# One selective scan in a fused layer: from 16 state rows over channels to tiles of 8 channels x 16 states, fed from DRAM and multiplied on GpSimd

## The chip, the cores and the metric

The kernel runs on one core of a Trainium2 chip. The metric is the time of one execution on the device, in microseconds (us): the median of three runs. Beside it there is one profiled execution, whose trace is what the rows below are read from. Engines are called PE (TensorE), DVE (VectorE), ACT (ScalarE), POOL (GpSimd) and SP (the queue that issues the transfers).

## The reference, cut to what matters

A layer of three parts runs over 16 sequences of 256 tokens with 128 channels: an attention with features instead of a softmax, a selective scan ("mixer") with a gated linear unit, and after each of them a feed-forward part with weights and activations rounded to FP4. The change is in the scan, and in one clip of the attention's features.

```python
exp_arg = jnp.clip(proj * sqrt_2s - s, -20.0, 20.0)      # attention: the clip
prf = jnp.exp(exp_arg) * inv_sqrt_m
...
def _selective_scan(u, dt, A, Bm, Cm, D):                # u, dt: [b, l, 256]; A: [256, 16]
    dA = jnp.exp(dt[..., None] * A)                      # decay
    dBu = (dt * u)[..., None] * Bm[:, :, None, :]        # drive; Bm, Cm: [b, l, 16]
    def step(h, inp):
        dA_t, dBu_t = inp
        h = dA_t * h + dBu_t
        return (h, h)
    ...
    y = jnp.einsum('lbdn,bln->bld', hs, Cm)              # read-out, summed over the 16 states
    return y + u * D
```

For each sequence that is 256 channels x 16 states = 4096 recurrences over 256 tokens.

## The kernel before, in words

A group is two sequences (512 tokens, `TOK`); there are 8 groups. The program is written out as ten turns of a software pipeline. A turn works on three groups at once: `new` (its attention), `mid` (attention's end, feed-forward A, mixer up to dt), `old` (the scan, mixer's end, feed-forward B). Each turn has two halves of 16 slots. In the first half DVE scans the old group while the feed-forward A of the middle group runs; in the second half the features, scores and context of the new group run, with the mixer of the middle group and feed-forward B of the old one. The order on every engine is the order of the code; engines meet at semaphores alone.

A sum over groups therefore has eight scan stretches: six in turns 2 to 7, which repeat with one period, one in turn 8 (no new group) and one in turn 9 (the last group alone, with some feed-forward work of the group before it).

The scan before lays 128 channels on the partitions and takes one state after the other. For each state `s`:

- `decay_in` (ACT, L705): exp(dt * -A) for both halves of the channels, from `dt` in SBUF into `decay`.
- `drive_by_token` (ACT, L717): dt*u, turned to tokens on partitions, times the B of that state.
- `drive` (PE, L1464): eight transposes bring it back into PSUM, banks 4 and 5.
- `scan` (DVE, L1147): two scans of 512 columns. Its first input `decay` is in SBUF, its second, the drive, is in PSUM; it writes `state` in SBUF.
- `read_out` (POOL, L623): `state` times the C of that state (`c_row`, loaded from DRAM to all partitions) into `read`, one multiply of 1024 columns. Before each of them `vector_rest` makes POOL wait until certain DVE instructions are done.
- `sum_states` (PE, L1480): the identity times `read`, summed over the states in banks 6 and 7.

Of the rest the text names: `features` (DVE), which clips `expf` (L1130) and multiplies it by `sqf` into `feat` (L1136); `hidden_*` and `ffn_input_*` (DVE), the rounding steps L1035, L1040, L1045, L1063 and L1116; `deviation` (POOL), which makes a normalisation's factors with a power (L559); the scaling of `qk` (DVE, L1219); the bias added to `xab` (POOL, L640) and the Newton step for `rnorm` (POOL, L648 to L657); `scale_hidden` (POOL, L576 to L585), which stands in the last turn only.

## Time and profile before

| | |
|---|---|
| median of 3 runs | 1380.71 us (1379.58 to 1384.39) |
| the profiled execution's own time | 1384.66 us |
| its span | 1382.6 us |
| busy share PE, DVE, ACT, POOL | 81%, 74%, 68%, 31% |
| instructions PE, DVE, ACT, POOL | 5421, 1576, 1829, 353 |
| moved by DMA | 41.11 MB, mean 30 GB/s |
| POOL's multiply by C (L623) | 128 times, 2359 ns each |
| DVE's scan (L1147) | 256 times, 1203 ns each |

The span runs from the first to the last instruction of the program; the profiled execution's own time is a little longer. Busy shares are means over the whole span, and the two halves of a turn differ: what limits one does not limit the other. An engine's idle time counts only where something later waits for it.

### The profile page before, as it was taken

Reading aid. Unit: us, or ns where it says so; the run is one execution under the profiler, and the core shown is the slowest. Engines: PE = TensorE matmul, PEld = TensorE weight load, DVE = VectorE, ACT = ScalarE, POOL = GpSimd, SP = SyncE. Lnnn points to the kernel's source line nnn. Section 1 sums busy time; section 2 is a strip of 40 time slices with the busy share of each in tenths; the row PEclk is TensorE's granted clock in tenths of the full one; section 3 lists DMA queues with packets and bytes.
Section 4 is the critical chain, followed back from the end, with each engine's and each line's share of the span. In section 5 each row is a group of like instructions: output and inputs, shape, how many; then the busy total and the mean of one; then the engine's idle time right before and its main releaser. Section 6 shows DMA issues by size and latency. Waiting matters only on the chain. (4 is left out here: it accounts for less than half of the span.)

```text
span 1382.6 us, 17127 instructions
## 1 busy us (share of the span) xinstructions
PE 1117.1 (81%) x5421; PEld 620.8 (45%) x5421; DVE 1018.5 (74%) x1576; ACT 937.3 (68%) x1829; POOL 422.6 (31%) x353
## 2 busy tenths in 40 slices
PE   3975788798888988898889888899779887856854
PEld 1343444444544455544544454544545454424423
DVE  1655658877897789887887789887887788646643
ACT  3443579767795769667886769577886768457721
POOL 3010106520354006520354006510443015404623
PEclk8786899999999999999999999999999999967885
DMA  2000012100110102101120002000110101000200
GB/s 73 1 3 6 1 32 61 40 1 32 32 62 15 32 1 69 39 1 32 33 67 8 32 1 77 31 1 32 39 54 9 32 15 62 23 32 28 60 12 8
DMA packets 31401, 41.11 MB, mean 30 GB/s; under 512 B 4617, under 2 KB 14674, under 8 KB 31314
## 3 DMA queue, kind: packets, MB, share of 16 engines
q1 hardware_dynamic: 31314, 40.02, 9.7%
q8 instruction: 46, 0.75, 0.2%
q14 instruction: 41, 0.34, 0.1%
HBM read 37.65 MB, written 2.36 MB: 29 GB/s over the span
## 5 line engine op out<-in xcount | busy, mean ns | idle before, releaser
L623 POOL TENSOR_TENSOR read<-state,c_row 128x1024 f32<-128x1024 f32 x128 | 300.4, 2359 | 280.0 <-DVE state L1147 107.8
L1147 DVE TENSOR_TENSOR_SCAN state<-decay,bank 128x512 f32<-128x512 f32 x256 | 296.2, 1203 | 56.5 <-PE bank L1464 47.5
L1480 PE MATMUL bank<-read,ident 128*128 128x512 f32 x512 | 258.8, 634 | 1.1 <-POOL read L623 1.1
L1464 PE MATMUL bank<-ident,drive_by_token 128*128 128x128 f32 x1024 | 167.7, 302 | 99.2 <-DVE state L1147 90.6
L717 ACT ACTIVATE drive_by_token<-dtu_t,b_t 128x256 f32<-128x256 f32 x512 | 217.3, 500 | 1.0 <-PE bank L1464 0.9
L1464 PEld LDWEIGHTS bank<-ident,drive_by_token 128*128 128x128 f32 x1024 | 124.2, 152 | 165.4 <-issue 108.6
L705 ACT ACTIVATE decay<-dt,neg_a 128x510 f32<-128x510 f32 x256 | 169.6, 713 | 12.5 <-DVE state L1147 12.5
L1405 PE MATMUL bank<-znt,omega 128*128 128x512 f32 x256 | 141.0, 633 | 22.1 <-ACT sqf L696 22.0
L1157 DVE TENSOR_TENSOR s_sb<-bank,causal 128x512 f32<-128x512 f32 x128 | 88.0, 688 | 78.0 <-PE bank L1418 77.8
L693 ACT ACTIVATE expf<-bank,minus_s,root2s 128x512 f32<-128x512 f32 x128 | 99.6, 778 | 65.7 <-PE bank L1405 64.7
L1480 PEld LDWEIGHTS bank<-read,ident 128*128 128x128 f32 x512 | 98.0, 208 | 86.3 <-issue 80.3
L1442 PE MATMUL bank<-s_sb,vext 128*32 128x256 f32 (+1 forms) x1024 | 128.8, 342 | 0.9 <-ACT s_sb L726 0.5
L551 POOL TENSOR_SCALAR a_ln_rstd<-a_ln_mv 128x4 f32<-128x4 f32 x8 | 1.6, 194 | 405.4 <-DVE a_ln_mv L1017 405.4
L1416 PE MATMUL bank<-feat 64*128 64x256 f32 x512 | 94.1, 430 | 16.1 <-ACT s_sb L726 16.1
L726 ACT ACTIVATE s_sb<-bank 128x256 f32<-128x256 f32 x128 | 49.3, 385 | 78.1 <-DVE s_sb L1157 78.1
L1136 DVE SCALAR_TENSOR_TENSOR feat<-expf,scale_f,sqf 128x512 f32<-128x512 f32 x128 | 96.2, 752 | 6.4 <-ACT sqf L696 0.5
L1442 PEld LDWEIGHTS bank<-s_sb,vext 128*32 128x32 f32 x1024 | 39.8, 110 | 92.6 <-issue 59.8
L1416 PEld LDWEIGHTS bank<-feat 64*128 64x128 f32 x512 | 42.5, 186 | 76.8 <-issue 61.2
L696 ACT ACTIVATE sqf<-bank 128x512 f32<-128x512 f32 x128 | 75.9, 593 | 0.0
L1130 DVE TENSOR_SCALAR expf<-expf 128x512 f32<-128x512 f32 x128 | 57.9, 452 | 18.1 <-ACT expf L693 17.6
L1405 PEld LDWEIGHTS bank<-znt,omega 128*128 128x128 f32 x256 | 43.6, 196 | 59.4 <-issue 54.3
L1418 PEld LDWEIGHTS bank<-feat 64*128 64x128 f32 x512 | 55.6, 191 | 3.6
(235 smaller groups left out, 1721.8 us busy)
## 6 DMA issues: line engine op xcount, KB each, us to landing
c_row<-c_rows SPq DMA_DIRECT2D x128, 256.0 KB, 3.2
xa<-x_dram SPq DMA_DIRECT2D x8, 256.0 KB, 3.8
out_dram<-x SPq DMA_DIRECT2D x8, 256.0 KB, 2.4
omega<-omega_t_dram SPq DMA_DIRECT2D x1, 512.0 KB
c_rows<-xdbl SPq DMA_DIRECT2D x8, 32.0 KB, 1.6
wqkv<-w_qkv_t_dram SPq DMA_DIRECT2D x1, 192.0 KB
state<-w_down_dram SPq DMA_DIRECT2D x1, 176.0 KB, 2.7
state<-w_gate_dram SPq DMA_DIRECT2D x1, 128.0 KB, 2.0
```

The costliest lines, as they stand in the source:

```text
L623: pool.tensor_tensor(read[:, s % STATE_BUFFERS], state[:, s % STATE_BUFFERS], c_row[:, s % C_BUFFERS].unsqueeze(1).broadcast_to([P, DT, TO ...
L693: act.activation(expf[:, s % 2], bank[:, 0], ACT.Exp, bias=minus_s[:], scale=root2s[:]).then_inc(exp_done.sem, 1)
L705: last = act.activation(decay[:, s % 2, k, :, 1:], dt[:, k].rearrange("p (b t) -> p b t", b=SEQS)[:, :, 1:], ACT.Exp, scale=neg_a[:, k, s: ...
L717: last = act.activation(by_token[:, s % DRIVES, t], dtu_t[:, t], ACT.Identity, scale=b_t[:, t, s:s + 1])
L1136: dve.scalar_tensor_tensor(feat[:, s % 2], expf[:, s % 2], scale_f[:], sqf[:, s % 2], ALU.mult, ALU.mult).then_inc(feat_done.sem, 1)
L1147: dve.tensor_tensor_scan(state[:, s % STATE_BUFFERS, c], decay[:, s % 2, c].rearrange("p b t -> p (b t)"), bank[:, DRIVE_BANK + c], 0.0, A ...
L1157: dve.tensor_tensor(s_sb[:, s % S_BUFFERS].rearrange("p h (k t) -> p h k t", t=P)[:, :, 0:3:2], bank[:, 1:3, 0:SEQ + P].rearrange("p h (k ...
L1405: pe.matmul(bank[:, 0], omega[:, j], znt[:, b], start=True, stop=True).then_inc(proj_ps.sem, 1)
L1416: pe.matmul(bank[:, 1 + h, 0:SEQ], f[:, SEQ:SEQ + P], f[:, 0:SEQ], start=True, stop=True)
L1442: last = pe.matmul(o, columns, scored, start=(k == 0 and below == 0), stop=(k == 1 and below == 1))
L1464: last = pe.transpose(bank[:, DRIVE_BANK + c, t * P:(t + 1) * P], by_token[:, s % DRIVES, t, c * P:(c + 1) * P], ident[:])
L1480: last = pe.matmul(bank[:, 6 + k], ident[:], read[:, s % STATE_BUFFERS, k], start=(s == 0), stop=(s == STATES - 1))
```

## The change

Eight channels x 16 states lie on the 128 partitions now, so one scan of 512 columns advances 8 channels with all their states. 32 such tiles cover the 256 channels; two of them make a span, and there are 16 spans for a group, one to a slot as the states were. The scans are as many as before and of the same length, but both their inputs lie in SBUF.

- `dt` and `dt*u` are stored to DRAM (`store_dt`), and each span loads its rows from there, each row to 16 partitions: `load_dt` into `decay`, `load_dtu` into `state`, 128 x 1024 each. B and C come from DRAM once for a group (`load_bc`).
- POOL multiplies a span by B in place (`drive`) and, after the scan, by C in place (`read_out`). The drives run `LEAD` = 5 spans ahead. `vector_rest` is gone.
- ACT makes the decay in place, and zeroes two columns first. Its multiply by B and PE's transposes of the drive are gone.
- PE sums the states with 0/1 tiles (`pick`) of 32 columns instead of the identity.
- The clip of `expf` stays on DVE for the first three slots (`CLIPS`) and is done on POOL in the other 13.
- dt is made on DVE in slot 10 instead of 12. Three small DVE instructions change their form (from one tensor input and two numbers to two tensor inputs).

```diff
@@ scan()
                 dve.wait_ge(decay_done.sem, decay_done.at(gb, s + 1))
-
-                dve.wait_ge(read_done.sem, read_done.at(gb, max(s + 1 - STATE_BUFFERS, 0)))
-                for c in range(DT):
-                    dve.wait_ge(drive_ps.sem, drive_ps.at(gb, DT * s + c + 1))
-                    dve.tensor_tensor_scan(
-                        state[:, s % STATE_BUFFERS, c],
-                        decay[:, s % 2, c].rearrange("p b t -> p (b t)"),
-                        bank[:, DRIVE_BANK + c], 0.0, ALU.mult, ALU.add).then_inc(
-                            (half_done if c == 0 else state_done).sem, 1)
+                dve.wait_ge(drive_done.sem, drive_done.at(gb, s + 1))
+                for e in range(2):
+                    span = state[:, s % STATE_BUFFERS, e]
+                    last = dve.tensor_tensor_scan(
+                        span, decay[:, s % DECAY_BUFFERS, e].rearrange("p b t -> p (b t)"), span,
+                        0.0, ALU.mult, ALU.add)
+                last.then_inc(state_done.sem, 1)
...
@@ GpSimd: drive, read_out, clip
+            def in_place(span, rows):
+
+                return pool.tensor_tensor(span, span, rows[:].unsqueeze(1).broadcast_to(
+                    [P, 2, TOK]), ALU.mult)
+
+            def drive(group, s):
+
+                landed = state_loaded[s % STATE_BUFFERS]
+                pool.wait_ge(bc_loaded.sem, bc_loaded.at(group, 2))
+                pool.wait_ge(landed.sem, landed.at(group, s // STATE_BUFFERS + 1))
+                in_place(state[:, s % STATE_BUFFERS], b_rows).then_inc(drive_done.sem, 1)
+
+            def read_out(group, s):
+
                 pool.wait_ge(state_done.sem, state_done.at(group, s + 1))
...
-                vector_rest(turn, s)
...
+                in_place(state[:, s % STATE_BUFFERS], c_rows).then_inc(read_done.sem, 1)
...
+            def clip(ga, s):
+
+                pool.wait_ge(exp_done.sem, exp_done.at(ga, s + 1))
+                pool.wait_ge(clipped.sem, clipped.at(ga, s))
+                pool.tensor_scalar(expf[:, s % 2], expf[:, s % 2], EXP_HIGH, EXP_LOW,
+                                   ALU.min, ALU.max).then_inc(clipped.sem, 1)
...
@@ SP: the loads of a span
+            def load_dt(group, s):
+
+                sp.wait_ge(dt_stored.sem, dt_stored.at(group, DT))
+                sp.wait_ge(state_done.sem, state_done.at(group, s + 1 - DECAY_BUFFERS))
+                slot = s % DECAY_BUFFERS
+                sp.dma_start(decay[:, slot].rearrange("p e b t -> p (e b t)"),
+                             span_rows(dt_dram, s)).then_inc(decay_loaded[slot].sem, 16)
...
@@ ACT: decay_in
+                act.activation(rows[:, :, 1, 0], rows[:, :, 1, 0], ACT.Copy, scale=0.0)
+                for e in range(2):
+                    last = act.activation(rows[:, e, :, 1:], rows[:, e, :, 1:], ACT.Exp,
+                                          scale=neg_a[:, tile_of(s, e):tile_of(s, e) + 1])
...
@@ PE: sum_states (and drive() is gone)
-                for k in range(DT):
-                    last = pe.matmul(bank[:, 6 + k], ident[:], read[:, s % STATE_BUFFERS, k],
-                                     start=(s == 0), stop=(s == STATES - 1))
+                k, q = divmod(s // 2, WIDE // CHANNELS)
+                for e in range(2):
+                    g = 2 * (s % 2) + e
+                    last = pe.matmul(bank[WIDE * g:WIDE * (g + 1), 6 + k], pick[:, q],
+                                     state[:, s % STATE_BUFFERS, e], start=(q == 0),
+                                     stop=(q == WIDE // CHANNELS - 1))
```

**The order on POOL.** These are POOL's instructions from the end of a second half into the next first half, in the kernel before: the factors of feed-forward B's and of the attention's normalisation, then the multiplies by C.

```order
156 L551 TENSOR_SCALAR b_ffn_ln_rstd<-b_ffn_ln_mv 128x4
157 L555 TENSOR_SCALAR b_ffn_ln_shift<-b_ffn_ln_mv 128x4
158 L559 TENSOR_TENSOR b_ffn_ln_rstd<-b_ffn_ln_rstd,minus_half 128x4
159 L566 TENSOR_TENSOR b_ffn_ln_shift<-b_ffn_ln_shift,b_ffn_ln_rstd 128x4
160 L551 TENSOR_SCALAR a_ln_rstd<-a_ln_mv 128x4
161 L555 TENSOR_SCALAR a_ln_shift<-a_ln_mv 128x4
162 L559 TENSOR_TENSOR a_ln_rstd<-a_ln_rstd,minus_half 128x4
163 L566 TENSOR_TENSOR a_ln_shift<-a_ln_shift,a_ln_rstd 128x4
164 L623 TENSOR_TENSOR read<-state,c_row 128x1024 x2
```

And the same place now:

```order
277 L700 TENSOR_SCALAR expf<-expf 128x512 x7
278 L649 TENSOR_TENSOR state<-state,b_rows 128x1024
279 L700 TENSOR_SCALAR expf<-expf 128x512
280 L649 TENSOR_TENSOR state<-state,b_rows 128x1024
281 L700 TENSOR_SCALAR expf<-expf 128x512
282 L649 TENSOR_TENSOR state<-state,b_rows 128x1024
283 L700 TENSOR_SCALAR expf<-expf 128x512
284 L649 TENSOR_TENSOR state<-state,b_rows 128x1024 x2
285 L649 TENSOR_TENSOR state<-state,c_rows 128x1024
286 L608 TENSOR_SCALAR a_ln_rstd<-a_ln_mv 128x4
```

The clips of slots 13, 14 and 15 stand behind the first three multiplies by B, and the attention's normalisation of the next group stands behind two more of them and one multiply by C.

**The order on DVE.** This is DVE at the end of the second half and the start of the first, in the kernel before; then now.

```order
616 L1040 SCALAR_TENSOR_TENSOR b_ffn_rounded<-b_ffn_magic,b_ffn_h 128x704
617 L1045 SCALAR_TENSOR_TENSOR b_ffn_rounded<-b_ffn_magic,b_ffn_rounded 128x704
618 L1116 TENSOR_TENSOR b_ffn_h<-b_ffn_rounded,b_ffn_qh_scale 128x704
619 L1147 SCALAR_TENSOR_TENSOR state<-decay,bank 128x512 x2
620 L1167 TENSOR_SCALAR rden<-bank 128x32
```

```order
551 L1074 SCALAR_TENSOR_TENSOR b_ffn_rounded<-b_ffn_magic,b_ffn_h 128x704
552 L1079 SCALAR_TENSOR_TENSOR b_ffn_rounded<-b_ffn_magic,b_ffn_rounded 128x704
553 L1150 TENSOR_TENSOR b_ffn_h<-b_ffn_rounded,b_ffn_qh_scale 128x704
554 L1181 SCALAR_TENSOR_TENSOR state<-decay,state 128x512 x4
555 L1200 TENSOR_SCALAR rden<-bank 128x32
```

Four scans stand there now instead of two (the scan is printed under its instruction's kind), and the second input of each is `state` instead of `bank`.

## Rows read from the trace of the kernel before

**Rows 1.** Busy time by half: a second half of a turn, then the next first half

```profile
core 0: us, PE busy (x) PEld busy (x) DVE busy (x) ACT busy (x) POOL busy (x), PEclk, DMA share, GB/s
591.00:669.70 78.70, 71.21 (x390) 35.97 (x388) 61.60 (x107) 57.88 (x106) 6.83 (x12) 0.98 0.05 15
669.70:744.60 74.90, 62.18 (x287) 38.71 (x288) 65.77 (x93) 58.37 (x123) 42.52 (x29) 0.95 0.18 50
...
1200.00:1280.00 80.00, 52.00 (x175) 28.20 (x174) 41.59 (x64) 48.99 (x92) 24.86 (x21) 0.72 0.09 27
```

**Rows 2.** DVE instructions with two SBUF inputs beside POOL: timeline, one turn

```profile
561.69 3.25 DVE L1219 TENSOR_TENSOR qk<-qk,rnorm 128x512 f32<-128x512 f32 x2
...
561.43 2.35 POOL L623 TENSOR_TENSOR read<-state,c_row 128x1024 f32<-128x1024 f32 x1
```

**Rows 3.** The same by line: duration ns min/median/max over the span

```profile
L1219 DVE TENSOR_TENSOR qk<-qk,rnorm x16: 678/686/2681, 29.8 to 1025.2; 128x512 f32<-128x512 f32 x16
...
L559 POOL TENSOR_TENSOR b_ffn_ln_rstd<-b_ffn_ln_rstd,minus_half x8: 1007/1523/1525, 309.8 to 1338.4; 128x4 f32<-128x4 f32 x8
...
L1147 DVE TENSOR_TENSOR_SCAN state<-decay,bank x256: 1186/1196/1222, 207.3 to 1320.6; 128x512 f32<-128x512 f32 x128
...
L623 POOL TENSOR_TENSOR read<-state,c_row x128: 2340/2358/2379, 214.9 to 1321.9; 128x1024 f32<-128x1024 f32 x128
```

**Rows 4.** POOL's and DVE's groups in one first half (busy us, mean ns)

```profile
L623 POOL TENSOR_TENSOR read<-state,c_row 128x1024 f32<-128x1024 f32 x16 | 37.5, 2357 | 26.9 <-DVE x L1124 6.5 <-DVE a_ffn_h L1116 6.2 <-DVE a_ffn_h L1035 4.6
L640 POOL TENSOR_TENSOR xab<-xa,bout 128x512 f32<-128x512 f32 x1 | 1.3, 1276 | 0.0
...
L1147 DVE TENSOR_TENSOR_SCAN state<-decay,bank 128x512 f32<-128x512 f32 x32 | 37.0, 1203 | 4.6 <-PE bank L1464 4.6
```

**Rows 5.** Busy time of tile newton_t, of tile a_ffn_rounded on DVE, of line L1035

```profile
669.70:744.60 74.90, 1.61 (x4) 0.95 0.18 50
...
669.70:744.60 74.90, 7.99 (x9) 0.95 0.18 50
...
669.70:744.60 74.90, 2.48 (x3) 0.95 0.18 50
```

**Rows 6.** The end of a second half: tile b_ffn_rounded, then a group of DVE

```profile
656.00:669.80 13.80, 2.68 (x3) 0.00 (x0) 0.88 0.00 0
...
L1136 DVE SCALAR_TENSOR_TENSOR feat<-expf,scale_f,sqf 128x512 f32<-128x512 f32 x2 | 1.5, 751 | 0.1
```

**Rows 7.** Timeline: DVE near the end of the second half; POOL's last multiply, two turns

```profile
645.89 0.68 DVE L1157 TENSOR_TENSOR s_sb<-bank,causal 128x512 f32<-128x512 f32 x1
...
589.51 2.35 POOL L623 TENSOR_TENSOR read<-state,c_row 128x1024 f32<-128x1024 f32 x1 [3.26 <-DVE state L1147]
...
743.14 2.35 POOL L623 TENSOR_TENSOR read<-state,c_row 128x1024 f32<-128x1024 f32 x1 [3.27 <-DVE state L1147]
```

**Rows 8.** Timeline of the last two turns: POOL, and DVE's dt*u

```profile
1202.53 2.34 POOL L623 TENSOR_TENSOR read<-state,c_row 128x1024 f32<-128x1024 f32 x1 [2.82 <-DVE state L1147]
...
1245.68 1.23 DVE L1338 TENSOR_TENSOR dtu<-dt,u 128x1024 f32<-128x1024 f32 x1
...
1266.72 2.60 POOL L576 TENSOR_SCALAR b_ffn_magic<-b_ffn_magic 128x704 bf16<-128x704 bf16 x1 [6.46 <-DVE b_ffn_rounded L1040]
...
1271.03 1.39 POOL L585 TENSOR_TENSOR b_ffn_h<-b_ffn_rounded,b_ffn_qh_scale 128x704 f32<-128x704 f32 x1
...
1321.86 2.34 POOL L623 TENSOR_TENSOR read<-state,c_row 128x1024 f32<-128x1024 f32 x1 [2.10 <-DVE state L1147]
```

**Rows 9.** Transfers: issues (KB each, us to landing), and the queue (packets, MB, share)

```profile
c_row<-c_rows SPq DMA_DIRECT2D x128, 256.0 KB, 3.2
...
out_dram<-x SPq DMA_DIRECT2D x8, 256.0 KB, 2.4
...
q1 hardware_dynamic: 31314, 40.02, 9.7%
```

**Rows 10.** POOL's one-input instruction of the Newton step, 128x128

```profile
L654 POOL TENSOR_SCALAR newton_t<-newton_t x8: 305/305/972, 28.9 to 1021.5; 128x128 f32<-128x128 f32 x8
```

More of the change, by code:

```diff
@@ new lines, in store_dt, with span_rows @@
+            def store_dt(group, values, dram, done, stored_in):
+                sp.wait_ge(done.sem, done.at(group, 1))
+                sp.wait_ge(state_done.sem, state_done.at(group, 0))
+                per = WIDE // CHANNELS
+                for k in range(DT):
+                    sp.dma_start(dram[per * k:per * (k + 1)].rearrange("q d g t -> g (q d) t"),
+                                 values[:, k]).then_inc(stored_in.sem, 16)
+            def span_rows(dram, s):
+                row = P // WIDE * TOK
+                return bass.AP(dram.tensor, s // 2 * CHANNELS * row + s % 2 * 2 * TOK,
+                               [[row, CHANNELS], [0, STATES], [1, 2 * TOK]])
@@ L492, in _ @@
                 if turn.has_old:
-                    for s in range(C_BUFFERS, 2 * C_BUFFERS):
-                        load_c(turn.old, s)
+                    for s in range(DECAY_BUFFERS, STATE_BUFFERS):
+                        load_dt(turn.old, s)
                 if i + 1 < GROUPS:
@@ L497, in _ @@
                 if turn.has_old:
-                    for s in range(2 * C_BUFFERS, STATES):
-                        load_c(turn.old, s)
+                    for s in range(STATE_BUFFERS, SPANS):
+                        load_dtu(turn.old, s)
+                        load_dt(turn.old, s)
                 if turn.is_last:
@@ L662, in body @@
                     attention_rest(turn, k)
-                    if turn.has_old:
-                        read_out(turn, k)
+                    if turn.has_old and k + LEAD < SPANS:
+                        drive(turn.old, k + LEAD)
+                    if turn.has_old and k + 1 < SPANS:
+                        read_out(turn.old, k + 1)
                 if turn.has_mid:
                     deviation(norm_b, turn.mid)
-                if turn.has_old:
-                    deviation(ffn_b.norm, turn.old)
+                for k in range(SLOTS):
+                    if turn.has_new and k >= CLIPS:
+                        clip(turn.new, k)
+                    if turn.has_old and k == 5:
+                        deviation(ffn_b.norm, turn.old)
+                    if turn.has_mid and k >= SLOTS - LEAD + 1:
+                        drive(turn.mid, k - (SLOTS - LEAD + 1))
+                if turn.has_mid:
+                    drive(turn.mid, LEAD - 1)
+                    read_out(turn.mid, 0)
                 if turn.is_last:
@@ L854, in mixer_early @@
                     ffn_ht(ffn_b, old, 0)
-                if turn.has_mid and k == 14:
-                    for h in range(DT):
-                        act.wait_ge(dtu_t_ps.sem, dtu_t_ps.at(mid, h + 1))
-                        act.activation(
-                            dtu_t[:, 2 * h:2 * h + 2].rearrange("p t c -> p (t c)"),
-                            bank[:, 4 + h], ACT.Copy).then_inc(dtu_t_done.sem, 1)
             def mixer_rest(turn, k):
@@ L1352, in body @@
                 for k in range(SLOTS):
-                    if turn.has_old and k > 0:
-                        scan(turn.old, k)
+                    if turn.has_old and 1 < k + 1 < SPANS:
+                        scan(turn.old, k + 1)
                     if turn.has_mid and k == 0:
@@ L1369, in body @@
                     mixer_rest(turn, k)
+                    if turn.has_mid and k == SLOTS - 1:
+                        scan(turn.mid, 0)
                 if turn.has_mid:
-                    scan(turn.mid, 0)
+                    scan(turn.mid, 1)
                 if turn.is_last:
@@ L1689, in body @@
                         gates(ffn_a, mid, 0)
-                    if turn.has_old and k + 1 < STATES:
-                        drive(old, k + 1)
                     if turn.has_mid and k == 6:
@@ L1710, in body @@
                 if turn.has_old:
-                    sum_states(old, STATES - 2)
-                if turn.has_old and not turn.has_new:
-                    sum_states(old, STATES - 1)
+                    sum_states(old, SPANS - 1)
                 if turn.has_new:
@@ L1762, in _, with tile_of @@
             turns(pe, body)
-SUMS = ((), ()) + tuple((s,) for s in range(11)) + ((11, 12), (), (13,))
+SUMS = ((), (), (0,), (1, 2)) + tuple((s,) for s in range(3, 15))
+def tile_of(span, e):
+    rows = WIDE // CHANNELS
+    return P // CHANNELS * (span // 2 // rows) + rows * (2 * (span % 2) + e) + span // 2 % rows
 def heads_of(pair):
@@ L1785 @@
 LOADS = 16
-BUILT = 9 + 2 + 3 + 2 + 1
+BUILT = 11 + 4 + 3 + 2 + 1
 DERIVED = 9
```

288 lines of the change are left out of this document (118 added, 170 removed).

## The prediction

> **What bounds the kernel now.** I read first the busy time of the two halves of a turn [rows 1]. In a second half PE is busy 71.2 of 78.7 us: it sets the pace there. In a first half DVE has the most work, 65.8 of 74.9 us, PE 62.2, ACT 58.4, and POOL only 42.5. By these rows the change looks good: it takes work off PE, ACT and DVE and gives it to POOL, the idlest engine. So the question is what POOL's instructions cost the others, and I read next the timeline of DVE and POOL side by side. There the reader is to see a DVE instruction that stands still. POOL's multiply runs from 561.43 to 563.78; DVE starts the two `qk` multiplies at 561.69 and is through at 564.94, so both were done in the 1.16 us after POOL's end [rows 2]. Over the whole span this instruction takes 0.69 us in the median and up to 2.68 [rows 3]. Both its inputs lie in SBUF. It works the other way too: POOL's power L559 takes 1.01 us at best, 1.52 in the median, where DVE is at its two-input `u` when POOL comes to it [rows 3]. But the scan, with one input in PSUM, ran beside POOL's multiplies all the time, and neither shows it: 1.19 to 1.22 us over 256 scans, 2.34 to 2.38 over 128 multiplies [rows 3]. So one thing in SBUF is shared by POOL and those DVE instructions that read two tensors there, and one waits until the other is through. The scan of before is not among them. The scan of after has both inputs in SBUF, and POOL has twice as many multiplies.
>
> **The sum.** I take the stretch from a group's first multiply by B to its last multiply by C, and add up everything in it that needs the shared thing.
>
> *Its start.* dt is made in slot 10: behind the mask that ends at 646.6 [rows 7] come dt and dt*u, 1.23 us each as in [rows 8], to 649.0. The store lands after 2.4 us, as the output's does. A load of 256 KB lands after 3.2 us; the queue moved 40.02 MB in 9.7% of 1382.6 us, 298 GB/s, so the second 256 KB of a span's rows take 0.9 more: 4.1 us [rows 9]. The first drive starts at about 655.5. The two slots by which dt comes earlier pay for this path.
>
> *POOL's part.* 16 multiplies took 37.5 us [rows 4], 32 take 75.0. `xab` 1.3 [rows 4], the Newton step 1.6 [rows 5]. Three clips stand behind the first drives (slots 13 to 15). No row shows such a clip. Below it lies the Newton step's 128x128 with 0.31 us [rows 10], above it the 128x704 in bf16 with 2.60 [rows 8], which is 1.9 for 512 columns. I take 0.7, near the first, since it is f32 as the clip is: 2.1. Together 80.0 us. POOL's powers on a few columns are left out; DVE runs beside them.
>
> *DVE's part.* 32 scans 37.0 [rows 4]. That is the price with PSUM; with SBUF it can hardly be less, since the recurrence is the same. The rounding of feed-forward A: its tile took 8.0 us, L1035 2.5 [rows 5]. The end of feed-forward B: 2.7 [rows 6] and one more L1035 of 0.8. `qk` 2 x 0.69 = 1.4 [rows 3]. Three `feat` of 0.75 = 2.3 [rows 6]. Together 54.7 us.
>
> 80.0 + 54.7 = 134.7 us, so the stretch ends at 655.5 + 134.7 = 790.2. In the kernel before it ended at 743.14 + 2.35 = 745.5 [rows 7]. That is +44.7 us in each of the six turns that repeat (period 743.14 - 589.51 = 153.6).
>
> *Turn 8.* No new group, so no `xab`, Newton step and `qk`: 134.7 - 4.3 = 130.4. It starts three periods after 655.5, at 1116.4, and ends at 1246.8; before, at 1202.53 + 2.34 = 1204.9 [rows 8]: +41.9.
>
> *Turn 9.* dt*u is done at 1246.9 [rows 8], the drive starts 6.5 us later at 1253.4. POOL: 75.0 and two `scale_hidden` of 5.7 (1266.72 to 1272.42) [rows 8], 86.4. DVE: scans 37.0, and L1035 and L1040 twice, some 3.5: 40.5. The end is 1380.3 instead of 1324.2 [rows 8]: +56.1.
>
> Sum: 6 x 44.7 + 41.9 + 56.1 = 366 us. The profiled execution took 1384.7 us, 4 us over the median of the runs: 1751, and 1747 for a median.
>
> **What costs or brings nothing.** PE loses its transposes and ACT its multiply by B. Both are covered: in the stretch they wait for POOL and DVE anyway. The 13 clips taken off DVE free it in the second half, where PE's 71.2 us set the pace; at most 78.7 - 71.2 gives 6 us a turn, at least nothing; I take nothing. The price of a late clip is counted: those of slots 13 to 15 queue behind drives that wait for their rows, and `feat`, scores and context wait for them, but that lies inside the stretch. ACT's zeroing of two columns is 16 short instructions a group on an engine with 16 us idle in a first half [rows 1]. PE sums with matmuls of the same 512 columns. The three DVE instructions that change form had to wait for POOL before as well. The loads are 32 x 0.52 MB a group, 56 us at 298 GB/s, inside 135; the four buffers of `decay` give a load 3 x 8 us.
>
> **The rule that the sum leans on.** The Trainium skill, SBUF — State Buffer, "SBUF: two separate sides", says it as a lock: a DVE instruction with two SBUF inputs and a GpSimd instruction that reads SBUF exclude each other for the whole of the instruction. The rows show that for multiplies and powers, and no row shows it for a scan. By that rule the scans' 37.0 us count as they do in my sum; if a scan with two SBUF inputs went beside POOL as the scan of before does, 37.0 would drop out. The GPSIMD Engine Reference (3.1) has the tightest loop over 512 elements at 0.77 us; three clips would be 2.3 by it.
>
> **The rivals.**
> - *The scan does not hold POOL off, and it comes out faster.* For it: the scans of [rows 3]. Then POOL's own 80.0 us set the stretch, 655.5 to 735.5, 10.0 earlier than now; turn 8, with 77.1, 11.4 earlier; turn 9 ends at 1339.8, 15.6 later. 1384.7 - 60 - 11.4 + 15.6 = 1329. Each us that POOL is held by DVE's other instructions gives back 8: it decides at about 7 us a stretch; all 18 of them would give some 1455, half of them 1390. Against it: both inputs are now where `qk`'s are.
> - *The same, but held by most of them*: 1390 to 1455, a little slower.
> - *The transfers set it.* If loads landed one by one like the 256 KB in 3.2 us, 16.8 MB would take 205 us a group: 70 more than the stretch's 134.7. Eight times that on top of the sum is 2310. For it: four times the bytes of before. Against it: 298 GB/s of the queue while it moved, and issues that don't wait for each other.
> - *The lock and a cold PE.* In 1200:1280 PE, busy 52 of 80 us, was granted 0.72 of the clock, against 0.98 in a second half [rows 1]. PE will idle longer in the first halves. If a second half began at such a clock and its mean fell to 0.92, its 71.2 us would be 76; if the waits around them stay, that is 5 us a turn, 1790 in all. It is inside my range, as a surcharge.
>
> **Numbers.** Lock as summed, 0.78; no lock and faster, 0.08; no lock and slower, 0.07; transfers, 0.04; none of these, 0.03. The bounds of the first: the clip at 1.9 us adds 29, 5% of the stretch in which neither engine has the shared thing adds 54, the clock 40: 1875. Downward, a held instruction is through 0.1 us sooner after its release than it takes alone (1.16 for 2 x 0.69 [rows 2]); 90 such changes a stretch are 80 us in all, and 6 us of relief in eight second halves 48: 1615. So 1615 to 1875. Faster by over 0.3% 0.08, within 0.3% 0.02, slower 0.90; 0.3% is about what a measurement of this kernel can tell from no change.
>
> **What the profile would show.** Right: the scan's duration spread from 1.2 to over 3 us, or POOL's multiply from 2.3 to 3.5; POOL and DVE both busy over 90% of first halves of some 115 to 120 us; PE below 60% there. A scan that stays at 1.2 us with its second input in SBUF, beside multiplies of 2.36, breaks the main step. So does a POOL that idles on the transfers of `state`. A clip of 1.9 us, or gaps in which both engines wait for ACT's decay, would put the time at the upper end.

## The result

The changed kernel takes 1931.24 us in the median of 4 runs (1906.46 to 1943.56), the kernel before 1380.16 beside it: a ratio of 1.3861 with a 95% interval of 1.3811 to 1.3911. It is slower, as forecast, but by 551 us instead of 367, and outside the range. Two of the four runs, the profiled one among them, are more than 1.5% above the fastest, and the ratio is that of the other two (1906.46 and 1924.19): by it the changed kernel stands at 1913 us, 533 over before, and still outside the range. The profiled execution took 1938.28 us with a span of 1936.6.

The page of the changed kernel: busy time, the 40 slices, the queue, and the chain that ended last.

```profile
PE 1038.1 (54%) x4301; PEld 489.6 (25%) x4301; DVE 1239.8 (64%) x1472; ACT 744.7 (38%) x1421; POOL 897.8 (46%) x589
...
PEclk8979566976679666786669766796669766655555
DMA  2000444025410343015510345014420245025520
...
q1 hardware_dynamic: 54098, 153.53, 28.3%
...
DMA 28%; DVE 20%; PE 19%; POOL 18%; issue 5%; ACT 5%; SPq 4%; POOLq 0%; DVEq 0%; ACTq 0%
DMA state<-dtu_rows 21%; POOL state L649 12%; DVE state L1181 8%; DMA dtu_rows<-tanh_x 5%; PE bank L1440 4%; PE bank L1477 2%; PE bank L1451 2%; SPq L520 2%; SPq L528 2%; DMA decay<-dt_rows 2%; DVE a_ffn_rounded L1079 1%; PE bank L1516 1%; PE bank L1505 1%; PE bank L1626 1%; PE bank L1432 1%
```

The reader is to see two things. PE and ACT, which were busy for 133 and 116 us of a turn of 153.6 [rows 1], have only 19% and 5% of the chain. And first place in the chain is held by DMA: 21% of the span is the wait for rows of `dtu` that POOL is to multiply, 5% the store of those rows. The queue moved 153.53 MB in 28.3% of 16 engines' span.

The costliest groups by line (busy us, mean ns, idle time before and who ended it), and then the durations min/median/max of the scan, the multiply by B and the clip:

```profile
L1181 DVE TENSOR_TENSOR_SCAN state<-decay,state 128x512 f32<-128x512 f32 x256 | 477.1, 1915 | 86.0 <-ACT decay L759 86.0
L649 POOL TENSOR_TENSOR state<-state,c_rows 128x1024 f32<-128x1024 f32 x128 | 360.6, 2820 | 60.5 <-DVE state L1181 60.5
L649 POOL TENSOR_TENSOR state<-state,b_rows 128x1024 f32<-128x1024 f32 x128 | 332.8, 2600 | 484.9 <-DMA state<-dtu_rows 484.9
L1171 DVE SCALAR_TENSOR_TENSOR feat<-expf,scale_f,sqf 128x512 f32<-128x512 f32 x128 | 95.6, 747 | 200.5 <-POOL expf L700 198.0
```

```profile
L1181 DVE TENSOR_TENSOR_SCAN state<-decay,state x256: 1190/1217/3410, 229.0 to 1866.3; 128x512 f32<-128x512 f32 x128
...
L649 POOL TENSOR_TENSOR state<-state,b_rows x128: 2337/2360/3310, 206.5 to 1857.6; 128x1024 f32<-128x1024 f32 x128
...
L700 POOL TENSOR_SCALAR expf<-expf x104: 612/612/966, 44.8 to 1549.6; 128x512 f32<-128x512 f32 x104
```

The scan's median is still 1217 ns, but its longest is 3410 where it was 1222, and its mean 1915 where it was 1203 [rows 3, 4]: the stall forecast for an instruction with two SBUF inputs. The clip takes 612 ns; 0.7 us was assumed. What was not forecast: POOL stands idle for 484.9 us before its multiplies by B, for `state<-dtu_rows`.

One turn in numbers. From the timeline of POOL: the last multiply by C of a group, the first by B of the next group, and that group's last by C.

```profile
789.78 2.37 POOL L649 TENSOR_TENSOR state<-state,c_rows 128x1024 f32<-128x1024 f32 x1 [1.16 <-DVE state L1181]
...
869.38 2.34 POOL L649 TENSOR_TENSOR state<-state,b_rows 128x1024 f32<-128x1024 f32 x1 [23.17 <-DMA state<-dtu_rows]
...
1013.14 2.36 POOL L649 TENSOR_TENSOR state<-state,c_rows 128x1024 f32<-128x1024 f32 x1 [1.16 <-DVE state L1181]
```

| | forecast | after |
|---|---|---|
| last multiply by C to the next first by B | 63.6 us (591.9 to 655.5) | 77.2 (792.15 to 869.38) |
| first by B to last by C, the stretch | 134.7 | 146.1 (869.38 to 1015.50) |
| the turn (before: 153.6 [rows 7]) | 198.3 | 223.3 |

So each repeating turn is 25.0 us longer than forecast, 13.6 in the start and 11.4 in the stretch. The chain of waits shows what the start is made of, and POOL's timeline how the rows arrive:

```profile
848.72 1.24 DVE tanh_x L1371
...
850.53 12.13 DMA dtu_rows<-tanh_x
```

```profile
877.95 2.35 POOL L649 TENSOR_TENSOR state<-state,b_rows 128x1024 f32<-128x1024 f32 x1 [5.54 <-DMA state<-dtu_rows]
...
886.47 2.34 POOL L649 TENSOR_TENSOR state<-state,b_rows 128x1024 f32<-128x1024 f32 x1 [5.47 <-DMA state<-dtu_rows]
```

The store of dt*u lands after 12.13 us, with that of dt just ahead of it (four stores of 256 KB in all), where 2.4 were assumed, and the spans' rows come 8.5 us apart (869.38, 877.95, 886.47), where 4.1 were assumed. The windows (busy us of each engine, the granted clock, then the share of 16 DMA engines and GB/s) say why: first the store, then the loads.

```profile
850.00:862.00 12.00, 5.29 (x24) 2.68 (x24) 3.71 (x5) 2.40 (x5) 0.00 (x0) 0.79 0.25 86
869.40:912.80 43.40, 23.48 (x120) 15.42 (x120) 27.70 (x37) 10.77 (x23) 20.34 (x12) 0.62 0.53 127
```

A share of 0.25 is as much as 4 engines of 16 busy all the time, a share of 0.53 as much as 8.5. The store's description in the code has an outermost dimension of 4 (`g (q d) t`, P // WIDE), that of a span's load one of 8 (`[row, CHANNELS]`). The stores kept a quarter of the engines busy, the loads about half. 16 pairs of loads at 8.5 us are 136 us a group, as long as the whole forecast stretch. The Trainium skill, DMA: Bandwidth & Descriptors, section "Why a DMA increments its semaphore by 16 and not by 1", has this rule: the number of engines is the largest up to 16 that divides the slowest dimension of both sides. By that rule the stores get 4 and the loads 8, and the trace agrees (0.25 and 0.53 of 16).

### The profile page after: what moved, and what is told of

It reads as the page before. It is cut to its first block, busy times and chain, and to the rows that moved or that the text cites. A ratio compares the mean times of both kernels' runs of the same rounds, so it can differ in the third digit from the quotient of the medians.

```text
span 1936.6 us, 14819 instructions
## 1 busy us (share of the span) xinstructions
PE 1038.1 (54%) x4301; PEld 489.6 (25%) x4301; DVE 1239.8 (64%) x1472; ACT 744.7 (38%) x1421; POOL 897.8 (46%) x589
## 3 DMA queue, kind: packets, MB, share of 16 engines
q1 hardware_dynamic: 54098, 153.53, 28.3%
## 4 chain that ended last, share of the span: by engine, by line
DMA 28%; DVE 20%; PE 19%; POOL 18%; issue 5%; ACT 5%; SPq 4%; POOLq 0%; DVEq 0%; ACTq 0%
DMA state<-dtu_rows 21%; POOL state L649 12%; DVE state L1181 8%; DMA dtu_rows<-tanh_x 5%; PE bank L1440 4%; PE bank L1477 2%; PE bank L1451 2%; SPq L520 2%; SPq L528 2%; DMA decay<-dt_rows 2%; DVE a_ffn_rounded L1079 1%; PE bank L1516 1%; PE bank L1505 1%; PE bank L1626 1%; PE bank L1432 1%
## 5 line engine op out<-in xcount | busy, mean ns | idle before, releaser
L649 POOL TENSOR_TENSOR state<-state,b_rows 128x1024 f32<-128x1024 f32 x128 | 332.8, 2600 | 484.9 <-DMA state<-dtu_rows 484.9
L1181 DVE TENSOR_TENSOR_SCAN state<-decay,state 128x512 f32<-128x512 f32 x256 | 477.1, 1915 | 86.0 <-ACT decay L759 86.0
L1505 PE MATMUL bank<-state,pick_channels 128*32 128x512 f32 x512 | 196.8, 908 | 424.9 <-POOL state L649 412.3
L649 POOL TENSOR_TENSOR state<-state,c_rows 128x1024 f32<-128x1024 f32 x128 | 360.6, 2820 | 60.5 <-DVE state L1181 60.5
L1171 DVE SCALAR_TENSOR_TENSOR feat<-expf,scale_f,sqf 128x512 f32<-128x512 f32 x128 | 95.6, 747 | 200.5 <-POOL expf L700 198.0
L700 POOL TENSOR_SCALAR expf<-expf 128x512 f32<-128x512 f32 x104 | 65.6, 630 | 313.2 <-ACT expf L746 310.8
L759 ACT ACTIVATE decay<-decay,neg_a 128x510 f32<-128x510 f32 x256 | 168.9, 709 | 0.0
L1440 PE MATMUL bank<-znt,omega 128*128 128x512 f32 x256 | 154.7, 690 | 11.4 <-ACT sqf L749 11.4
L1505 PEld LDWEIGHTS bank<-state,pick_channels 128*32 128x32 f32 x512 | 21.3, 130 | 539.4 <-POOL state L649 452.6
L757 ACT ACTIVATE decay<-decay 128x2 f32<-128x2 f32 x128 | 26.1, 204 | 272.0 <-DMA decay<-dt_rows 271.8
L1551 PE MATMUL bank<-wdown,b_ffn_ht 128*128 128x128 f32 x180 | 42.0, 420 | 106.2 <-DVE b_ffn_h L1104 103.8
L749 ACT ACTIVATE sqf<-bank 128x512 f32<-128x512 f32 x128 | 75.6, 590 | 0.0
L1551 PEld LDWEIGHTS bank<-wdown,b_ffn_ht 128*128 128x128 f32 x180 | 38.1, 319 | 113.6 <-issue 108.7
```

The lines of the kernel that those rows point to most:

```text
L649: return pool.tensor_tensor(span, span, rows[:].unsqueeze(1).broadcast_to([P, 2, TOK]), ALU.mult)
L749: act.activation(sqf[:, s % 2], bank[:, 0], ACT.Square).then_inc(sq_done.sem, 1)
L759: last = act.activation(rows[:, e, :, 1:], rows[:, e, :, 1:], ACT.Exp, scale=neg_a[:, tile_of(s, e):tile_of(s, e) + 1])
L1171: dve.scalar_tensor_tensor(feat[:, s % 2], expf[:, s % 2], scale_f[:], sqf[:, s % 2], ALU.mult, ALU.mult).then_inc(feat_done.sem, 1)
L1181: last = dve.tensor_tensor_scan(span, decay[:, s % DECAY_BUFFERS, e].rearrange("p b t -> p (b t)"), span, 0.0, ALU.mult, ALU.add)
L1440: pe.matmul(bank[:, 0], omega[:, j], znt[:, b], start=True, stop=True).then_inc(proj_ps.sem, 1)
```

## The experiments

Behind each median stand the ratio to the kernel before on the same chip and its 95% interval. All ratios are formed as that of the changed kernel above; for it and for e5 they stand lower than the medians do, and where the two tell different sizes both are given. The lines of POOL's multiplies and of the scan have other numbers in some of these kernels (L638 for L649, L1176 or L1177 for L1181), and of every edit only the lines that matter are shown.

### e1 and e2: rows on all 16 engines, one direction at a time

e1 puts 128 rows outermost in the stores (and lets tiles take channels in natural order, so that a store is the plain tile; the addresses of the loads, `a_log` and `pick` follow):

```diff
-        of_span = (DT * WIDE // CHANNELS, CHANNELS, P // WIDE, TOK)
+        of_span = (DT, P, TOK)
...
-                    sp.dma_start(dram[per * k:per * (k + 1)].rearrange("q d g t -> g (q d) t"),
-                                 values[:, k]).then_inc(stored_in.sem, 16)
+                    sp.dma_start(dram[k], values[:, k]).then_inc(stored_in.sem, 16)
```

e2 puts the 16 states outermost in the loads (and so on the partitions, with `a_log`, the rows of B and C and `pick_channels` to match), and leaves the stores:

```diff
-                               [[row, CHANNELS], [0, STATES], [1, 2 * TOK]])
+                               [[0, STATES], [row, CHANNELS], [1, 2 * TOK]])
```

Expected of e1: 

> The changed kernel (1931 us), with dt and dt*u stored to DRAM channel by channel, 128 rows outermost instead of 4, and loaded with 8 rows outermost as before; a span takes 16 channels in a row. In the changed kernel's trace the four stores took 12.1 us with some 4 packets in flight, and dt*u waited for them in each of the 8 groups. Theory A (transfers with few rows outermost run on that many DMA engines): the stores take 2.5 to 4 us and 16 packets are in flight, 8 x 8 to 9.5 us go, 1855 to 1870. Rival (the stores are slow because they scatter 2 KB rows over DRAM, or because dt*u's multiply is late): stores stay above 8 us, above 1900.

Expected of e2: 

> The changed kernel with the states outermost on the partitions instead of the channels, so that a load of a span has 16 rows outermost instead of 8; the stores stay at 4. Theory A: 16 packets in flight instead of 8.3 and over 200 GB/s instead of 125; a pair of loads in 4.2 us instead of 8.5; the first drive 2 to 4 us earlier, and the stretch from first drive to last read-out 135 us instead of 146, since POOL and DVE keep each other off (lock theory): 1800 to 1835. Rival B (the source rows, read 16 times each, limit the rate): still about 125 GB/s, above 1900. Rival C (no lock, the transfers set all of the stretch): the stretch falls below 110 us, under 1650.

Measured, two runs each: e1 1856.64 us (1.3445, 1.3403 to 1.3486), e2 1849.51 (1.3393, 1.3347 to 1.3439). The first came as expected, e2 gained less than forecast. By POOL's multiplies in the same turn as above:

| us | after | e1 | e2 | e3, below |
|---|---|---|---|---|
| last by C to next first by B | 77.2 | 68.0 | 75.6 | 63.2 |
| the stretch | 146.1 | 145.5 | 135.9 | 135.5 |

The slow stores lengthen the start, the slow loads the stretch and a little of the start. In e1 a 256 KB store now lands after 2.3 us, as the output's did [rows 9]; the row gives KB and median us to landing.

```profile
dtu_rows<-tanh_x SPq DMA_DIRECT2D x16, 256.0 KB, 2.3
```

e1 changes two things about a store: the dimension that stands outermost, and where its rows of 2 KB go in DRAM (scattered before, one after the other now). Its time alone can't tell the two apart. For the number of engines speak the share of 0.25 above and the counts of packets below e3.

### e3: both

The edits of e1 and e2 together; nothing of what is computed changes.

Expected: 

> Both: stores with 128 rows outermost, loads with 16. This is the changed kernel as the prediction had it, with transfers at the price that the trace of before suggested. Lock theory: first drive 6 to 8 us after dt*u, stretch of 133 to 140 us, scans still up to 3.4 us: 1735 to 1770, the predicted 1747. Rival C (transfers alone made it slow): 1380 to 1450. Rival D (a colder PE makes up the rest): above 1790.

Measured: 1756.64 us (1.2715, 1.2685 to 1.2746). POOL's timeline of one turn, and the windows of the time in which the first spans are loaded, of the stretch, and of what follows it:

```profile
791.97 2.34 POOL L638 TENSOR_TENSOR state<-state,b_rows 128x1024 f32<-128x1024 f32 x1 [11.93 <-DMA state<-dtu_rows]
...
796.34 2.35 POOL L638 TENSOR_TENSOR state<-state,b_rows 128x1024 f32<-128x1024 f32 x1 [1.33 <-DMA state<-dtu_rows]
...
925.12 2.36 POOL L638 TENSOR_TENSOR state<-state,c_rows 128x1024 f32<-128x1024 f32 x1 [1.16 <-DVE state L1176]
```

```profile
792.00:812.00 20.00, 12.72 (x70) 8.47 (x72) 8.71 (x14) 5.72 (x12) 13.80 (x8) 0.69 1.04 240
...
792.00:927.50 135.50, 82.03 (x255) 34.99 (x256) 117.26 (x110) 44.88 (x95) 102.83 (x48) 0.74 0.52 122
927.50:991.20 63.70, 57.97 (x282) 26.92 (x281) 44.44 (x74) 47.13 (x82) 11.14 (x21) 0.95 0.13 39
```

The share of DMA engines is 1.04, the rate 240 GB/s instead of 127, and the rows come 4.4 us apart. The pages count packets over the whole span; here are the changed kernel, e1, e2 and e3:

```profile
DMA packets 54177, 154.47 MB, mean 80 GB/s; under 512 B 4745, under 2 KB 14802, under 8 KB 54098
...
DMA packets 54561, 154.47 MB, mean 83 GB/s; under 512 B 5129, under 2 KB 15186, under 8 KB 54482
...
DMA packets 56353, 154.48 MB, mean 84 GB/s; under 512 B 6921, under 2 KB 16978, under 8 KB 56274
...
DMA packets 56737, 154.48 MB, mean 88 GB/s; under 512 B 7305, under 2 KB 17362, under 8 KB 56658
```

All that is added is packets under 512 B: 384 in e1, which is 12 for each of 32 stores, 2176 in e2, which is 8 for each of 272 loads (256 of spans, 16 of B and C), and 2560, the sum of both, in e3. One small packet for each engine of a transfer would give just these numbers if the stores went from 4 engines to 16 and the loads from 8 to 16. That is inferred; no row names the engines.

The stretch is 135.5 us (134.7 forecast), the rest of the turn 63.7 (63.6 forecast). With the transfers as the prediction had priced them, the kernel takes nearly what the prediction said, 1756.6 against 1747. The next runs ask whether it does so for the reasons given.

### e4: the scan's second input from PSUM

```diff
-                        span, decay[:, s % DECAY_BUFFERS, e].rearrange("p b t -> p (b t)"), span,
-                        0.0, ALU.mult, ALU.add)
+                        span, decay[:, s % DECAY_BUFFERS, e].rearrange("p b t -> p (b t)"),
+                        bank[:, 4 + e], 0.0, ALU.mult, ALU.add)
```

On top of e3. The multiply by B is made, but its values are not used: the kernel leaves B out.

Expected: 

> As e3_full, but the scan's second input is read from PSUM (banks 4 and 5, whatever stands there) instead of the driven state, so that it has one SBUF input as in the kernel before. The multiply by B is still made and waited for, only its values are not used. Lock theory: scans all at 1.19 to 1.22 us beside POOL's multiplies; the stretch falls from 135 to 85 to 105 us, 1400 to 1500 by the prediction's rival sum with most of DVE's other two-input instructions still held. Rival (the lock is a small part and POOL's doubled work or the waits on ACT set the stretch): within 3% of e3_full.

Measured: 1586.60 us (1.1499, 1.1466 to 1.1533), 170 less than e3 but more than forecast. Duration of the scan, min/median/max, and the windows of a stretch and of what follows:

```profile
L1176 DVE TENSOR_TENSOR_SCAN state<-decay,bank x256: 1185/1195/1221, 215.7 to 1514.2; 128x512 f32<-128x512 f32 x128
```

```profile
731.30:846.50 115.20, 72.40 (x246) 32.68 (x246) 91.71 (x107) 43.47 (x93) 86.44 (x48) 0.79 0.62 143
```

No scan is held any more (1221 ns at most, as before), and the stretch falls by 20.3 us to 115.2. By the prediction's sum, which counts each scan in full, it should have fallen by 37.0 to 97.7. So the sum was right in total and not in its parts: taking the stall away gives back 20.3 us a stretch, not 37.0, and what is left is 17.5 us longer than POOL's 80.0 and DVE's other 17.7 together, for which the sum has no term. POOL's timeline shows waits of this kind; the longest:

```profile
756.49 2.35 POOL L638 TENSOR_TENSOR state<-state,c_rows 128x1024 f32<-128x1024 f32 x1 [4.93 <-DVE state L1176]
...
786.21 2.35 POOL L638 TENSOR_TENSOR state<-state,b_rows 128x1024 f32<-128x1024 f32 x1 [6.57 <-DMA state<-dtu_rows]
...
834.99 2.90 POOL L638 TENSOR_TENSOR state<-state,c_rows 128x1024 f32<-128x1024 f32 x1 [4.10 <-DVE state L1176]
```

At 756 POOL waits for DVE's first scans, at 786 for the rows of the ninth span, and at the end, where multiplies by C alone are left, for scans again. The wait for the ninth span follows from the order of the code. SP issues the next group's load of `x` (L457, its wait is L456) ahead of the loads of spans nine to sixteen, and waits with it until POOL has done `xab`. SP's waits and then the chain of waits show it:

```profile
SPq L456 <- POOL xab L665: 13.4, 1, 13.4
```

```profile
779.71 0.39 SPq L457
780.19 5.89 DMA state<-dtu_rows
```

POOL's multiply at this place waited 7.15 us in the changed kernel (938.79) and 6.01 in e3 (852.86) as well. What the kernel would gain with the load of `x` at another place was not tried.

### e5: PSUM for the scan, with the change's own transfers

The edit of e4 on the changed kernel; B is left out of what it computes here too.

Expected: 

> The changed kernel, with its own slow transfers, but the scan takes its second input from PSUM (a bank that is never driven with this group's data), so the multiply by B is made and not used: the output is not the reference's. Theory 'the loads are a bound of their own, just under the lock': 32 loads of 4.27 us are 137 us a group, so the stretch from first multiply by B to last by C falls only from 145 to some 137 to 142 and the start stays 19 us: 1840 to 1890 us. Rival 'the loads only delay the start': then the stretch is 115 us as in the run with fast rows, and only the start's 10.5 us a turn come on top of 1587: 1660 to 1700 us.

Measured: 1805.86 us (1765.94 to 1830.37; ratio 1.2858, 1.279 to 1.2927). By its ratio it stands at 1774 us. Either figure lies between the two forecasts, and the runs lie 64 us apart, so it settles less than the others. In the profiled run (1829.68) the stretch is 128.3 us in the turn shown and 120 to 140 in the eight of them: neither the 115 of e4 nor the steady 137 to 142 that were expected. So the slow loads alone keep the stretch above e4's, close under the stall.

```profile
815.70:944.00 128.30, 69.65 (x254) 34.12 (x254) 90.88 (x106) 44.44 (x94) 84.20 (x48) 0.62 0.43 130
```

```profile
L649 POOL TENSOR_TENSOR state<-state,b_rows 128x1024 f32<-128x1024 f32 x128 | 307.5, 2402 | 511.0 <-DMA state<-dtu_rows 511.0
```

POOL is idle for 511.0 us for the rows, more than the 484.9 of the changed kernel: where the scans don't hold it, it waits for the loads.

### e6: all clips back on VectorE

`CLIPS = 16` instead of 3, on top of e3. DVE had stood idle for POOL's clips before `feat`, 198.0 us in the changed kernel and 77.8 still in e3.

Expected: 

> The variant with the fast rows in both directions (1756.6 us), with all 16 clips of exp back on VectorE as before. Theory A, clips queue on GpSimd behind multiplies by B that wait for their rows, and the features, scores and context with them: a turn gains up to the 9 us for which a feature was seen to wait, 1690 to 1740 us. Theory B, the prediction's (that wait lies inside the stretch, where GpSimd and VectorE's shared time is the bound; three clips fewer on GpSimd and three more, with one SBUF input, on VectorE): 1740 to 1760 us. If VectorE's 13 clips, some 0.4 us each, come on top of a second half: up to 1790 us.

Measured: 1751.87 us (1.2678, 1.2636 to 1.2720) against e3's 1.2715 (1.2685 to 1.2746): no difference that the intervals tell. The turn of the table takes 199.3 us in both: in e6 the stretch is 1.6 us shorter and the time to the next one 1.6 longer. So the 77.8 us of idle time before `feat` in e3 cost nothing that shows; the other 120 had gone with the slow transfers.

### e7: the stall alone, in the kernel before

```diff
-                        bank[:, DRIVE_BANK + c], 0.0, ALU.mult, ALU.add)
+                        dtu[:, c], 0.0, ALU.mult, ALU.add)
```

One operand of the scan, in the kernel before. The transposes are still made and waited for; B is left out of what the kernel computes.

Expected: 

> The kernel before with one edit: the scan reads its second input from dt*u in SBUF instead of from the PSUM bank (the transposes that fill the bank are still made and waited for; the multiply by B is so left out of the result, and the output is not the reference's). GpSimd's work, transfers and all instruction counts are those of before. Lock theory: the scans' durations spread to over 3 us and GpSimd's multiplies to over 3; of the 256 scans those beside a multiply by C are serialised with it. In a first half of 75 us GpSimd's 37.5 us, the scans' 37 and VectorE's other two-input work of 15 to 18 must then fit one after another, some 92: +15 to +20 us in each of seven or eight turns, 1480 to 1540 us. Rival (the scan is not held, and the spread seen after comes from the write of the in-place state or from contention of transfers): scans stay at 1.2 us and the time at 1380 to 1390 us.

Measured: 1549.20 us (1.1234, 1.1209 to 1.1259), 169 more than before, by a kernel with the same instructions, the same 16 multiplies a group and the same transfers. Duration of the scan and of the multiply by C, min/median/max; then the timelines of DVE and POOL at one place; then the windows of a turn:

```profile
L1147 DVE TENSOR_TENSOR_SCAN state<-decay,dtu x256: 1190/1218/3331, 201.7 to 1477.8; 128x512 f32<-128x512 f32 x128
...
L623 POOL TENSOR_TENSOR read<-state,c_row x128: 2338/3046/3327, 211.0 to 1479.0; 128x1024 f32<-128x1024 f32 x128
```

```profile
776.41 4.44 DVE L1147 TENSOR_TENSOR_SCAN state<-decay,dtu 128x512 f32<-128x512 f32 x2
```

```profile
776.73 3.05 POOL L623 TENSOR_TENSOR read<-state,c_row 128x1024 f32<-128x1024 f32 x1 [5.54 <-DVE a_ffn_h L1035]
```

```profile
651.00:737.50 86.50, 75.69 (x436) 40.86 (x434) 68.63 (x122) 63.09 (x118) 9.88 (x16) 0.98 0.04 14
737.50:826.20 88.70, 64.78 (x244) 37.24 (x243) 82.32 (x77) 53.81 (x112) 54.28 (x26) 0.85 0.13 42
```

DVE starts two scans at 776.41. POOL starts its multiply at 776.73, and it takes 3.05 us instead of 2.36 [rows 3]: 0.7 longer, where some 0.9 us were left of the first scan. The two scans take 4.44 us instead of 2.4: the second waits until POOL is through at 779.78, and ends 1.07 us later. That is the picture of `qk` in [rows 2], now on the scan, both ways. The turn is 175.2 us instead of 153.6 [rows 1].

### e8: the doubled multiplies of POOL

```diff
-                in_place(state[:, s % STATE_BUFFERS], b_rows).then_inc(drive_done.sem, 1)
+                one = state[:, s % STATE_BUFFERS, 0, 0:1]
+                pool.tensor_tensor(one, one, b_rows[:, 0:1], ALU.mult).then_inc(drive_done.sem, 1)
```

On top of e4: the multiply by B is cut to one column.

Expected: 

> The variant with fast rows and the scan's second input from PSUM (1586.6 us, 205 us over before), with the multiply by B cut down to one column, so that GpSimd has the 16 multiplies of before; the output is not the reference's. Theory 'the doubled work of GpSimd is the rest': the stretch falls from 115 us to some 80 to 85, the period to some 155 to 160, and the time to 1390 to 1440 us. Rival 'the rest is what comes ahead of the stretch, the trip of dt*u through DRAM, and PE's colder second halves': only 1500 to 1570 us.

Measured: 1448.06 us (1.0486, 1.0464 to 1.0509), 139 less than e4 and 8 above the forecast. The windows from the first scan to POOL's last multiply, and to the next first scan:

```profile
697.60:773.90 76.30, 51.59 (x166) 22.41 (x168) 68.45 (x93) 35.67 (x77) 47.18 (x40) 0.82 0.68 157
773.90:858.70 84.80, 73.26 (x372) 35.71 (x368) 56.05 (x92) 55.95 (x101) 13.43 (x28) 0.92 0.33 84
```

The turn is 161.1 us against 153.6 [rows 1]: 7.5 a turn are left for the change's remaining parts (the rows' way through DRAM, sums that start later, ACT's zeroing).

### e10: the stall with single multiplies, in the changed layout

The edit of e8 on top of e3, so the scan has two SBUF inputs and POOL 16 multiplies a group.

Expected: 

> The variant with fast rows (1756.6 us), the scan with both inputs in SBUF as in the change, and the multiply by B cut down to one column, so that GpSimd has only the 16 multiplies by C; the output is not the reference's. Lock theory, by the prediction's sum: 80.0 + 54.7 - 37.5 = 97 us for the stretch, against some 74 us of scans in the same kernel with PSUM, so that about the 22 us a turn that the lock alone added to the kernel before come on top of 1448 us: 1600 to 1630 us. Rival (the lock costs only where GpSimd is busy most of the stretch, with 32 multiplies): 1450 to 1530 us.

Measured: 1553.69 us (1.1252, 1.1231 to 1.1272), 106 over e8, in neither range: less than the stall costs in the kernel before (169, e7) and more than the rival allowed. The scan's group in e10, then in e7:

```profile
L1177 DVE TENSOR_TENSOR_SCAN state<-decay,state 128x512 f32<-128x512 f32 x256 | 371.7, 1504 | 34.9 <-ACT decay L749 34.9
```

```profile
L1147 DVE TENSOR_TENSOR_SCAN state<-decay,dtu 128x512 f32<-128x512 f32 x256 | 492.9, 1974 | 26.3 <-PE bank L1464 16.4 <-ACT decay L705 7.5 <-POOL read L623 2.3
```

The scan's mean is 1504 ns in e10 and 1974 in e7: in the mean a scan is held for less time there. The same 16 multiplies and 32 scans a group do not have one price; it depends on how they meet.

### e9: the clips alone, in the kernel before

The change's one part that takes work off DVE without giving it two SBUF inputs: 13 of 16 clips go to POOL, as in the change, in the kernel before. DVE's side of the edit (POOL gets the `clip` of the change):

```diff
-                dve.wait_ge(exp_done.sem, exp_done.at(ga, s + 1))
-                dve.tensor_scalar(expf[:, s % 2], expf[:, s % 2], EXP_LOW, EXP_HIGH,
-                                             ALU.max, ALU.min).then_inc(clipped.sem, 1)
+                if s < CLIPS:
+                    dve.wait_ge(exp_done.sem, exp_done.at(ga, s + 1))
+                    dve.tensor_scalar(expf[:, s % 2], expf[:, s % 2], EXP_LOW, EXP_HIGH,
+                                      ALU.max, ALU.min).then_inc(clipped.sem, 1)
```

Expected: 

> The kernel before with one edit: 13 of the 16 clips of exp go to GpSimd, in the second half, as in the changed kernel (0.61 us each there, one SBUF input). Theory A: they only lengthen the way from exp to features of a slot (VectorE's own clip is shorter and needs no change of engine), while PE's 71 us set the second half: 1380 to 1400 us. Rival: VectorE, busy 61.6 of 78.7 us in a second half, is late often enough that 13 instructions less give 2 to 5 us a turn: 1345 to 1370 us.

Measured: 1371.71 us in 7 runs (0.9940, 0.9917 to 0.9962). It is the fastest kernel of this study, 8 us below before: between the two forecasts, about 1 us a turn.

## Why the forecast came out as it did

In order, each with one thing more of the change (medians, and the steps by medians and by ratios):

| kernel | us | step | by ratios |
|---|---|---|---|
| before | 1380 | | |
| e8: rows through DRAM on 16 engines, 16 multiplies, scan from PSUM | 1448 | +68 | +67 |
| e4: 32 multiplies a group | 1587 | +139 | +140 |
| e3: scan from SBUF | 1757 | +170 | +168 |
| after: stores on 4, loads on 8 engines | 1931 | +175 | +158 |

- **The main step, the stall, was right in kind.** e7 shows it by a single operand, e4 takes it away by a single operand. The Trainium skill's rule (SBUF — State Buffer, "SBUF: two separate sides") that a DVE instruction with two SBUF inputs and a GpSimd instruction that reads SBUF exclude each other was shown for no scan by the rows of before. The scan of e7 agrees with it: 1218 ns in the median, 3331 at most.
- **The price of the transfers failed.** It stands in two places. "Its start" gave the store 2.4 us and a span's rows 4.1, from `out_dram` and `c_row` and the queue's 298 GB/s [rows 9]; measured were 12.13 and 8.5 us. "What costs or brings nothing" put the loads of a group at 56 us, covered by the stretch, from the same 298 GB/s; at 8.5 us a pair they are 136. The descriptions of `out_dram` and `c_row` have 128 rows outermost on both sides; the new transfers have 4 and 8 outermost on the DRAM side. The 298 GB/s come from 9.7% of 16 engines' span, so they are a rate with all 16 engines at work. By the same formula the changed kernel has 153.53 MB in 28.3% of 1936.6 us, 280 GB/s: the rate of an engine was priced nearly right, and the number of engines was not asked for. e3, with the dimensions in another order (and the channels placed to match), takes away 174.6 of the 184 us by which the forecast was short (by ratios 158 of 166).
- **The stretch was right in total by errors that cancel.** POOL's 80.0 and DVE's 54.7 us were added as if neither engine ever waited for anything else. e4 gives back 20.3 us for the stall of the scans where 37.0 were counted, and leaves 17.5 us for which nothing was; POOL is busy 86.4 us there instead of 80.0, and waits of 4 to 7 us stand in it. The agreement of 135.5 with 134.7 is therefore partly luck, and so is that of the whole: e3's last multiply by C ends 368 us later than before's (1692.6 against 1324.2 [rows 8]), where the sum had 366.
- **The rival of the transfers** was put at 0.04, with "against it: 298 GB/s of the queue while it moved". It named the right place, but for transfers that land one after the other (3.2 us per 256 KB, 70 us a turn). The truth was between: 8.5 us for the 1 MB of a pair, 2.1 for 256 KB, mostly beside the stall. Its other argument, issues that don't wait for each other, holds only in part: those of spans nine to sixteen stand behind SP's wait for `xab` (e4). It should have had more weight, and the range a bound for it.
- **The signs.** The scan's spread and the multiply's (3.31 us at most by B) came, and PE is at 48% of a stretch (70.08 of 146.1). POOL and DVE over 90% did not come: 67% and 76% (97.42 and 110.54 of 146.1), and 76% and 87% in e3. And POOL did idle on the transfers of `state`, the sign that the text itself had named as the one that breaks the step.
- **What was put at nothing.** Of PE's fewer transposes, ACT's fewer multiplies and DVE's fewer clips only the clips were run alone: 8 us less in the kernel before (e9), nothing that shows in e3 (e6). The other two were not. PE's granted clock fell further than the rival of the cold PE had it: 0.63 in the stretch shown and 0.87 (58.84 us busy of 77.3) between it and the stretch ahead of it, where a second half had 0.98 [rows 1]. In e3, where the waits for rows are shorter, it is 0.95 between two stretches. What the clock costs of the 175 us was not measured apart.

```profile
792.10:869.40 77.30, 58.84 (x286) 27.55 (x282) 44.42 (x74) 47.30 (x82) 11.18 (x23) 0.87 0.11 31
869.40:1015.50 146.10, 70.08 (x256) 33.55 (x256) 110.54 (x110) 45.15 (x95) 97.42 (x48) 0.63 0.41 114
```

Left open: how the 68 us of e8 divide; why the transfers' 175 us are more than e1's 75 and e2's 82 together (by ratios 158, 57 and 65; in the turn of the table it is the start, 9.2 and 1.6 us apart and 14.0 together); and the 17.5 us that e4 leaves in a stretch, whose longest waits were located, not removed.

## What to carry to other kernels

Before pricing a transfer by another's rate, compare the outermost dimension of both sides: here 4 and 8 there went with the work of 4 and 8 of 16 DMA engines, in transfers of 256 and 512 KB. Read the DMA share of a window times 16, and ask of a rate taken from a busy share how many engines it supposes. Moving an elementwise operand from PSUM to SBUF is not free where GpSimd works beside VectorE; one operand of a scan cost 12% here. A sum that comes out right has not yet been shown right: take away one term and see whether its own size goes.

## What the runs showed of the hardware

- Stores with 4 rows outermost ran at a share of 0.25, loads with 8 at 0.53 and 127 GB/s, loads with 16 at 1.04 and 240 GB/s, with the same bytes and the same issue queue.
- A scan with two SBUF inputs and a GpSimd multiply hold each other off: 3.41 us at most for the scan (1.22 before), 3.31 for a multiply by B (no multiply by C took over 2.38 before). With one input in PSUM the scan stays within 1185 to 1221 ns beside 256 multiplies.
- The same stall cost 105.6 us (e8 to e10), 169 (before to e7), 170 (e4 to e3) and 125 (e5 to after; 138 by ratios), by what else the two engines waited for.
